# Inverse square roots by powers on GpSimd, the second FFN product in three f32r parts, and a new order of steps in a graph attention kernel

## The chip, the core and the metric

The kernel runs on one core of one Trainium2 chip, in one launch. The metric is the device time in microseconds, median of the runs. A core has TensorE (PE; its weight loads are PEld), VectorE (DVE), ScalarE (ACT), GpSimd (POOL), and SyncE (SP), which here only issues DMAs. Each engine takes its instructions in the order written and waits on semaphores for the others.

## The reference

There are N = 10000 nodes with 512 features and E = 5000 edges, sorted by `dst`. Only the first block is run (one layer), and its result is normalized once more:

```python
q = (h @ Wq).reshape(n, 8, 64); k = (h @ Wk).reshape(n, 8, 64); v = (h @ Wv).reshape(n, 8, 64)
e = einsum('ehd,ehd->eh', k[src], q[dst]) / sqrt(64)
ex = exp(e - segment_max(e, dst)[dst]);  attn = ex / segment_sum(ex, dst)[dst]
a = segment_sum(attn[:, :, None] * v[src], dst).reshape(n, 512)
x1 = layernorm(h + a @ Wo, ln1_g, ln1_b)
f = relu(x1 @ W1 + b1) @ W2 + b2            # 512 -> 64 -> 512
y = layernorm(x1 + f, ln2_g, ln2_b)
out = layernorm(h + y)                      # no gain or bias; eps 1e-5 everywhere
```

A layer norm needs 1/sqrt(var + eps) of each row, three times for each node.

## The kernel before

**Rounds.** The edges are taken in ten rounds of 500 (four tiles of 125 rows). In a round the rows x[dst] and x[src] are gathered by indirect DMAs (`GXD`, `GXS`, four each), turned on TensorE (`TXD0` to `TXD3`, `TXS0` to `TXS3`, line 1023), and split into a rounded part and a rest in the f32r type (ScalarE line 519, VectorE line 759). The products with Wq, Wk, Wv and Wo (`Q0`..`Q3`, `K`, `V`, `O`; line 963) are each 4 chunks x 3 f32r matmuls (hi x hi, lo x hi, hi x lo). Softmax over a segment is done by scans along the edges (lines 784, 802, 838). `H0`..`H3` (line 821) add x[dst] to the O product.

**Jobs.** All that follows attention is done in four slots a round: N0 and N1 take nodes that no edge reaches (250 rows each), E0 and E1 take the rows of the edges. A slot's pass is called a job, so there are 40. Its steps are: `sum`/`mv` or `m1` (mean), `sd` (deviation), `r1` (reciprocal), `norm`, `T` (turning on TensorE, line 1059), `F1` (first FFN product, plain f32, line 1095), `F2` (second, plain f32: two matmuls with 64 rows of contraction, one on partitions 0 to 63 and one on 64 to 127, each into its own bank, line 1103), `xr`, `x2` (line 898, adds the FFN's result), `sq` (squares, line 558), `t`, `r2`, `y` (line 917), `sq3`, `r3`, `z` (the last norm) and `out` (two scatters). GpSimd issues all gathers and scatters, and `be`, a DMA that adds ln2's bias.

**The deviations.** ScalarE computes Sqrt(var + eps) of a 125x2 tile (line 550) and VectorE its reciprocal (line 856). Exp and Ln are in another table set than Sqrt, so that each round loads a set before its softmax (line 521) and the other one after it (line 533).

**The FFN's banks.** For a job ScalarE seeds one bank with zeros (line 609) and one with the bias (line 610); after `F1` it takes Relu with bias b1 into `hT` (line 600) and then seeds the first bank with the bias (line 602). The last three jobs have steps of their own (`B9`, `F19`, `F29`, lines 1072 to 1088).

**The start.** The indices are cast, turned by three small transposes (`TURN`, lines 972 and 975), and written to tables (`TABS`, line 675 and on). `TABS` stands behind all casts and behind `FLAG` on VectorE. GpSimd's constants (lines 398 to 409) stand ahead of `GXD`. SyncE issues the loads of Wq and Wk before those of b1 and W1, and that of Wv when the x[dst] rows are there. `COUNT0`..`COUNT4` (line 999), `ROFF` and `LIST` make the list of the nodes without an edge.

**The order.** `PLAN` gives each step of each engine a due time; `sequence(engine)` sorts by them, and the engine's block issues the steps in that order. Rounds 2 to 7 of the ten share one set of times, shifted by a period. `FILLERS` names steps behind which TensorE does idle matmuls on `below` (line 1116): 27 are in the start and in the closing jobs, 31 behind steps of round 8.

Of the kernel before, what the change touches and what calls it, by code (L numbers as in the profile page):

```python
# [21 lines left out]
PERIOD = 7684  # L22
SLOT_PERIOD = {"N0": 7687, "N1": 7689}
PLAN = {
    "pe": """
!TURN -276034; !FOLD -51782; !OFFS -237181; !TURNF -205187; !COUNT0 -202748; !COUNT1 -198663; !COUNT2 -146723;
!COUNT3 -94502; !COUNT4 -90190; !ROFF -71911; !BITS -8816; TXD0 -189819 -22912 125030 125323 125345;
TXS0 -102406 26305 131951 131437 131817; Q0 -138628 34546 131782 132194 129672; K0 -59911 65956 133983 133320 137209;
V0 27356 105501 136738 136738 170605; O0 89451 141151 143013 157654 247834; TXD1 -186065 -14365 126120 126712 125690;
TXS1 -100425 38188 132022 131705 131969; Q1 -106115 57936 132236 132221 132162; K1 -40813 69908 134313 133555 140512;  # L30
V1 33080 113889 136894 136880 181017; O1 106767 141614 143149 165755 248144; TXD2 -166405 -7868 129028 130799 126518;
TXS2 -88980 41299 132413 132381 134849; Q2 -86792 64359 132527 132551 134538; K2 -30166 75112 134486 134513 140777;
V2 33666 129876 137553 138275 190162; O2 109181 144067 143559 170305 254002; TXD3 -155949 21677 129100 130978 126648;
TXS3 -83495 62551 132620 132450 134986; Q3 -70414 73944 132661 132967 137118; K3 -18228 75867 134696 134659 145042;
V3 35699 134599 138141 140689 197551; O3 120150 144307 144103 175555 259059; S -2195 93578 135748 135731 159438;
<N0.T 145667 146316 145309 195433 299769; >N0.T9 136827 117852 145308 201617 306764;
>N0.B9 134375 173381 147765 210695 422904; >N0.F19 113824 134962 147690 188156 364727;
>N0.F29 123023 126945 148591 190152 461807; <N0.F1 147630 147818 147691 210881 382824;
<N0.F2 148607 149380 148592 224978 338963; N1.T 102574 142344 143517 152979 224183;
N1.F1 111204 143358 143969 159019 234579; N1.F2 115493 144385 144312 165751 254378;  # L40
<E0.T 122067 143089 144266 177444 355474; >E0.T9 160739 161239 144265 204642 261163;
>E0.B9 93219 141972 144577 202312 260912; >E0.F19 251340 193305 144554 229074 272138;
>E0.F29 116239 128247 144888 201657 275488; <E0.F1 141560 144900 144555 177658 271119;
<E0.F2 142460 145428 144889 179837 216780; <E1.T 143829 145481 144995 216690 280606;
>E1.T9 156254 161915 144994 210970 295480; >E1.B9 154640 155450 145824 230013 303813;
>E1.F19 150032 151466 145585 214520 312915; >E1.F29 121122 181510 146664 236757 339253;
<E1.F1 145525 146724 145586 230812 332624; <E1.F2 146622 147196 146665 235181 341159
""",
    "act": """
!HQ -295440; !HK -89319; !HV -61854; !HO -45097; TXD0 -171196 -18312 125712 127231 125178;  # L50
TXS0 -68603 20337 131158 130993 132478; Q0 -111138 42579 131621 131004 131070; V0 27197 127292 136963 137699 161962;
TXD1 -146012 -9176 126544 127368 125657; TXS1 -67208 29303 131398 131008 132770; Q1 -73839 60821 132277 131401 133090;
V1 37750 130738 138269 138390 173142; TXD2 -137214 -5075 128839 130614 126389; TXS2 -65419 35207 132157 131352 133268;
Q2 -17185 62273 132574 132889 134345; V2 62190 138918 139637 142583 207890; TXD3 -118766 8616 128915 130664 126472;
TXS3 -48877 52021 132497 132466 133316; Q3 -10791 71890 132992 133126 134392; V3 74728 140001 140381 145994 218182;
S 3247 92165 136014 135911 153062; LN 5242 95004 136180 136183 156284; XP 19875 106412 136396 136399 158334;
N0.sd 123676 144544 144342 152828 256165; N0.norm 139316 145803 144558 162385 274768;
<N0.T 145914 146124 145919 169837 375832; >N0.T9 183982 167878 145918 179401 296352;
>N0.F19 139706 158972 147088 149539 310138; <N0.seed 146645 147058 146583 176207 232821;
<N0.F1 147225 148612 147089 177596 315363; N0.sq 148176 149711 149081 215130 338403;  # L60
N0.sq3 150792 150053 150194 238119 450805; <N0.z 151547 150704 150711 263169 440476;
N1.sd 79021 140055 141467 142403 189027; N1.norm 95949 140381 142614 146272 196458;
N1.T 102191 142631 143102 147994 208475; N1.seed 77479 140669 142165 147282 218765;
N1.F1 109626 143603 143753 154439 220364; N1.sq 125334 145685 145585 156964 246118;
N1.sq3 143159 146401 146231 166158 297324; N1.z 146052 147623 148527 175369 319246;
E0.sd 116445 141882 143068 154716 239656; <E0.norm 130307 141972 143719 160108 226853;
<E0.T 133834 143647 144061 161814 186592; >E0.T9 200185 167176 144060 163787 257027;
>E0.F19 127976 159096 144422 167136 271087; <E0.seed 124355 144129 144234 162277 258999;
<E0.F1 140883 144817 144423 165883 237520; E0.sq 146290 146220 146119 168507 281215;
E0.sq3 147174 148677 147797 184383 337581; E0.z 147692 149932 149758 196327 349547;  # L70
E1.sd 132863 144633 144278 166339 260324; <E1.norm 136923 145071 144498 176344 204613;
<E1.T 143222 145930 144586 186840 203336; >E1.T9 157259 128692 144585 225796 279483;
>E1.F19 150692 123805 145647 214704 292567; <E1.seed 143985 146062 145367 199873 298615;
<E1.F1 144354 146133 145648 207445 312511; E1.sq 147924 147214 146670 227666 327598;
E1.sq3 148558 148885 149937 229129 359991; <E1.z 149166 150501 150260 232611 340778
""",
    "dve": """
!CAST -263381; !FLAG -243336; !TABS -242836; !FILLI -241863; !FW -55094; !B1 -55229; !LQ -172721; !LK -85485;
!LV -54432; !LO 76605; !CNT0 -198287; !CNT1 -179760; !CNT2 -159099; !CNT3 -97504; !CNT4 -91086; !RANK -79616;
!DIG -211902; !LIST -79575; TXD0 -162172 -29587 125840 127315 124482; TXS0 -89151 40059 130890 130776 132032;  # L80
K0 -51732 66249 133633 132533 134452; W0 18249 122663 136307 136222 169476; N0 35421 125323 136834 136488 170118;
G0 49521 129368 137409 137177 185919; L0 44048 128784 137153 137940 187035; H0 89910 140875 142983 151481 211814;
TXD1 -161904 -24476 126177 127482 124895; TXS1 -88968 56437 131385 130810 132286;
# [77 lines left out]
def graph_attention(nc, x, src, dst, Wq, Wk, Wv, Wo, g1, be1, g2, be2, W1, b1, W2, b2, out):  # L161
# [15 lines left out]
    with ctx:  # L177
# [125 lines left out]
        def hidden(i, slot):  # L303
            n = closing.index((i, slot))
            return pS[:, R * n:R * n + R]
# [4 lines left out]
        def pT_of(i, step, half=0):  # L310
            return pT[turn[i, step, half] % 2]
# [829 lines left out]
```

## Time and profile before

| | |
|---|---|
| three runs | 683.09, 683.85, 684.23 us; median 683.85 |
| profiled execution | span 682.0 us from first to last instruction; the page gives no separate device time for it, so that the median lies 1.85 us above this span |
| PE | 641.5 us busy, 94% |
| DVE | 578.0 us, 85% |
| ACT | 528.3 us, 77% |
| POOL | 401.7 us, 59% |
| DMA | 91.44 MB, mean 134 GB/s |
| granted TensorE clock | 0.986 on average |

Busy times are unions, so two instructions that run side by side count once. A group's mean is that of one instruction. A plain f32 matmul leaves two records in this profile and an f32r matmul one: the 80 F2 matmuls are 160 records, 12 of them in lines of the closing jobs.

### The profile page before, as it was taken

To read this page: it belongs to the slowest core of one execution; us is meant where nothing else is said; L and a number is where in the kernel's file an instruction comes from. 1 tells how busy PE (TensorE), PEld (TensorE's weight loads), DVE (VectorE), ACT (ScalarE), POOL (GpSimd) and SP (SyncE) were. 2 spreads that over 40 slices of the span, in tenths; PEclk is the share of its full clock that TensorE was granted. 3 is DMA by queue.
4 is the path that set the end of the run, shared out by engine and by line. 5 is a ranking of instruction groups with operands and counts; after the bars stand their busy time and mean duration, and the time that the engine had idled before them with its cause. 6 is when DMAs were issued, how large, how long until landed. Compare 5 with 4: busy or idle time off the path is not lost. (4 is left out here: it accounts for less than half of the span.)

```text
span 682.0 us, 10864 instructions
## 1 busy us (share of the span) xinstructions
PE 641.5 (94%) x3520; PEld 483.8 (71%) x3520; DVE 578.0 (85%) x1391; ACT 528.3 (77%) x1140; POOL 401.7 (59%) x363
## 2 busy tenths in 40 slices
PE   5999999999999999999999999999999999999950
PEld 2778877777777777777777777777778778675520
DVE  7668769879898898898889889988989898899792
ACT  2525269877888987988798889878878999698881
POOL 7267244867675865756776574864547726735423
PEclk9999999999999999999999999999999999999995
DMA  7844154644643745674474456455554824536452
GB/s 227 220 101 133 44 123 106 173 122 142 148 121 131 159 121 148 167 157 92 146 177 117 113 161 137 105 168 123 127 128 155 184 62 135 139 77 138 131 113 91
DMA packets 37747, 91.44 MB, mean 134 GB/s; under 512 B 8346, under 2 KB 9642, under 8 KB 37690
## 3 DMA queue, kind: packets, MB, share of 16 engines
q0 software_dynamic: 31536, 82.74, 47.6%
q1 hardware_dynamic: 6154, 8.01, 4.3%
q8 instruction: 28, 0.46, 0.3%
q14 instruction: 29, 0.24, 0.1%
HBM read 71.20 MB, written 20.99 MB: 135 GB/s over the span
## 5 line engine op out<-in xcount | busy, mean ns | idle before, releaser
L558 ACT ACTIVATE squares<-rows,nmean 125x512 bf16<-125x512 f32 x200 | 142.3, 713 | 41.5 <-DVE nmean L902 19.8
L412 POOL DMA_INDIRECT x_rows<-in_x_dram,node_idx x40 | 48.2, 1205 | 56.8 <-DVE rows L917 47.3
L416 POOL DMA_INDIRECT out_dram<-rows,node_idx x40 | 46.4, 1160 | 56.4 <-ACT rows L618 47.0
L473 POOL DMA_DIRECT2D x_rows<-in_L_gnn_ln_b_dram x40 | 52.9, 1372 | 31.1 <-DVE rows L821 21.7
L898 DVE SCALAR_TENSOR_TENSOR rows<-pF,rows 125x512 f32<-125x512 f32 x78 | 50.6, 686 | 23.2 <-PE pF L1103 22.5
L963 PE MATMUL pP<-wo_hi,aT_hi 128*125 128x512 f32 x160 | 65.9, 412 | 0.3 <-DVE aT_lo L848 0.3
L963 PE MATMUL pP<-xTs_hi,wv_hi 128*128 128x500 f32 x160 | 65.8, 411 | 0.0
L963 PE MATMUL pP<-xTd_hi,wq_hi 128*128 128x500 f32 x160 | 65.4, 409 | 0.1
L963 PE MATMUL pP<-xTs_hi,wk_hi 128*128 128x500 f32 x160 | 63.5, 397 | 0.6 <-ACT q L539 0.6
L963 PE MATMUL pP<-wo_lo,aT_hi 128*125 128x512 f32 x160 | 63.1, 394 | 0.0
L963 PE MATMUL pP<-wo_hi,aT_lo 128*125 128x512 f32 x160 | 63.0, 394 | 0.0
L416 POOL DMA_INDIRECT out_dram<-rows,edge_idx x40 | 43.5, 1086 | 33.1 <-ACT rows L618 23.8
L963 PE MATMUL pP<-xTs_hi,wk_lo 128*128 128x500 f32 x160 | 62.4, 390 | 0.0
L963 PE MATMUL pP<-xTs_hi,wv_lo 128*128 128x500 f32 x160 | 62.3, 390 | 0.0
L963 PE MATMUL pP<-xTd_lo,wq_hi 128*128 128x500 f32 x160 | 62.3, 390 | 0.0
L963 PE MATMUL pP<-xTd_hi,wq_lo 128*128 128x500 f32 x160 | 62.2, 389 | 0.0
L963 PE MATMUL pP<-xTs_lo,wv_hi 128*128 128x500 f32 x160 | 62.2, 388 | 0.0
L963 PE MATMUL pP<-xTs_lo,wk_hi 128*128 128x500 f32 x160 | 62.1, 388 | 0.0
L412 POOL DMA_INDIRECT x_rows<-in_x_dram,edge_idx x40 | 44.5, 1113 | 28.1 <-issue 11.3
L618 ACT ACTIVATE rows<-rows,shift,rs 125x512 f32<-125x512 f32 x76 | 57.4, 805 | 1.4 <-DVE shift L933 1.4
L917 DVE SCALAR_TENSOR_TENSOR rows<-rows,rs,x_rows 125x512 f32<-125x512 f32 x80 | 57.1, 750 | 0.9 <-DMA x_rows<-in_L_gnn_ln_b_dram 0.7
L907 DVE SCALAR_TENSOR_TENSOR rows<-rows,nmean,g_all 125x512 f32<-125x512 f32 x80 | 57.6, 761 | 0.1
(197 smaller groups left out, 1760.6 us busy)
## 6 DMA issues: line engine op xcount, KB each, us to landing
x_rows<-in_L_gnn_ln_b_dram POOLq DMA_DIRECT2D x40, 512.0 KB, 6.7
dst_row<-in_dst_dram SPq DMA_DIRECT2D x9, 250.5 KB
q<-in_L_gnn_Wq_dram SPq DMA_DIRECT2D x1, 1024.0 KB, 5.6
rows<-in_L_gnn_Wk_dram SPq DMA_DIRECT2D x1, 1024.0 KB, 7.8
rows<-in_L_gnn_Wv_dram SPq DMA_DIRECT2D x1, 1024.0 KB, 6.8
x_rows<-in_L_gnn_Wo_dram SPq DMA_DIRECT2D x8, 128.0 KB, 6.0
xd<-in_x_dram,dst_idx POOLq DMA_INDIRECT x40, 4.6
xs<-in_x_dram,src_idx POOLq DMA_INDIRECT x40, 3.8
```

The lines of the kernel that those rows point to most:

```text
L412: pool.indirect_dma_start(rows, None, x, bass.IndirectOffsetOnAxis(ap=table[:, column:column + 1].bitcast(U32), axis=0), bounds_check=N - ...
L416: pool.indirect_dma_start(out, bass.IndirectOffsetOnAxis(ap=table[:, column:column + 1].bitcast(U32), axis=0), rows, None, bounds_check=N ...
L473: pool.dma_start(xr_wide[n], bass.AP(tensor=be2.tensor, offset=be2.offset, ap=[[0, P], [0, 2], [1, D]]), accum_op=ALU.add).then_inc(s[f"be ...
L558: ins = act.activation(squares[:, t, :], w[n][:, t, :], ACT.Square, bias=nmean[c][n][:, t:t + 1], accum_out=sq[c][n][:, t:t + 1])
L618: ins = act.activation(w[n][:, t, :], w[n][:, t, :], ACT.Identity, scale=rs[3][n][:, t:t + 1], bias=shift[n][:, t:t + 1])
L898: dve.scalar_tensor_tensor(w[n][:, t, :], f_banks(i, slot)[t][0:R, :], 1.0, w[n][:, t, :], ALU.mult, ALU.add, accum_out=sums[2][n][:, t:t ...
L907: ins = dve.scalar_tensor_tensor(w[n][:, t, :], w[n][:, t, :], nmean[2][n][:, t:t + 1], g2_all[0:R, :], ALU.add, ALU.mult)
L917: ins = dve.scalar_tensor_tensor(w[n][:, t, :], w[n][:, t, :], rs[2][n][:, t:t + 1], xr[n][:, t, :], ALU.mult, ALU.add, accum_out=sums[3][ ...
L963: ins = pe.matmul(acc, left(a, k), right(b, k), start=(k == 0 and a == b), stop=(k == KC - 1 and a == 1))
```

## The change

**Powers on GpSimd.** `sd`, `r2` and the reciprocals of `r1` and `r3` go, and both table loads of each round. New POOL steps `p1`, `p2`, `p3` do two small instructions each: var = scale * x + eps, then var to the power -0.5. One table set is loaded at the start. The bias b1 is put into the seeded bank, so that Relu has none.

```diff
-    act.activation(sd[c][n][:, :], var, ACT.Sqrt, bias=eps_col[0:R, :], scale=scale).then_inc(s[f"sd{c}"], 1)
-    dve.reciprocal(rs[c][n][:, :], sd[c][n][:, :]).then_inc(s[f"rs{c}"], 1)
+    if what in ("p1", "p2", "p3"):                                    # GpSimd
+        if what == "p1" and slot[0] == "N":
+            on.wait_ge("mv_done", 2 * nth("dve.mv", slot, i))
+            pool.tensor_scalar(var[c][n][:, :], mv[n][:, :, 1], 1.0, EPS, ALU.mult, ALU.add).then_inc(s[f"var{c}"], 1)
+        else:
+            on.wait_ge(f"sq{c}", nth(f"act.sq{c}", slot, i))
+            pool.tensor_scalar(var[c][n][:, :], sq[c][n][:, :], 1.0 / D, EPS, ALU.mult, ALU.add).then_inc(s[f"var{c}"], 1)
+        on.wait_ge(f"var{c}", nth(f"pool.p{c}", slot, i))
+        pool.tensor_tensor(rs[c][n][:, :], var[c][n][:, :], minus_half[0:R, :], ALU.pow).then_inc(s[f"rs{c}"], 1)
-                act.preload_act_table_set(tables)
-                act.preload_act_table(ACT.Sqrt)
```

**F2 as three f32r products.** W2 is split into hi and lo at the start (`FHI` on ScalarE, `FLO` on VectorE), `hT` in each job (Relu writes hi, the new VectorE step `lo` the rest). The bank that `F1` used is seeded in a step of its own (`seed1`) behind `lo`.

```diff
-    for t in range(2):
-        pe.matmul(pF[1 - t][0:R, :], hT[DFF * t:DFF * t + DFF, :], w2[DFF * t:DFF * t + DFF, :], ...)
+    on.wait_ge("h_lo", nth("dve.lo", slot, i))
+    for a, b in ((0, 0), (1, 0), (0, 1)):
+        for t in range(2):
+            half = slice(DFF * t, DFF * t + DFF)
+            ins = pe.matmul(f_banks(i, slot)[t][0:R, :], hT[a][half, :], w2[b][half, :], start=False, stop=(b == 1), ...)
+    dve.scalar_tensor_tensor(hT[1][:, :], hidden(i, slot), 0.0, hT[0][:, :].bitcast(F32), ALU.max, ALU.subtract)
```

**Gathers first.** `TURN`, `CAST` and `TABS` are cut in two, so that the dst table is written right behind its own cast and transpose. `GXD` stands ahead of GpSimd's later constants (now step `INIT`), `GXS` behind them. SyncE issues Wk (and W2 ahead of it) when x[dst] is there, and Wv when x[src] is there.

**Tile-wise turning.** `TXDt` and `TXSt` now turn tile t (125 rows, all four chunks) and not chunk k of all tiles, and wait for that tile's gather alone; each gather of the next round waits for its own tile's turning.

```diff
-    on.wait_ge(f"{which}_loaded", 64 * (i + 1))
-    for t in range(4):
-        ins = pe.transpose(pT_of(i, step)[:, R * t:R * t + R], rows[0:R, t, P * k:P * k + P], ident[0:R, 0:R])
+    on.wait_ge(f"{which}_loaded_{t}", 16 * (i + 1))
+    for k in range(KC):
+        ins = pe.transpose(pT_of(i, step)[:, R * k:R * k + R], rows[0:R, t, P * k:P * k + P], ident[0:R, 0:R])
```

**The order.** `PLAN` has a time for each step of each of the ten rounds; the sum of the steps is the same but for those named. The due times are in another unit than before. The first PE steps are now TURN1, TURN2, OFFS, TURNF, TXD0, TXD1, TXD2, FOLD, TXD3, Q0, TXS0, COUNT0, COUNT1 (before: TURN, OFFS, TURNF, COUNT0, COUNT1, TXD0 to TXD3, COUNT2, Q0). Three closing jobs (E0, N0, E1 of round 9) still follow the last product O3. `FILLERS` now has 24 idle matmuls, all in the start.

**Smaller.** The row of dst values shares its memory with `weight`, and its load for the next round waits for `log_taken` instead of `mask_eq`. Of the three closing jobs E0 and E1 of round 9 keep `B9`; N0 goes the ordinary way. The index fill has one semaphore a round.

## Rows read from the trace of the kernel before

**Rows 1.** The page's first part: busy us, share of the span, instructions

```profile
PE 641.5 (94%) x3520; PEld 483.8 (71%) x3520; DVE 578.0 (85%) x1391; ACT 528.3 (77%) x1140; POOL 401.7 (59%) x363
```

**Rows 2.** Stretches of the span; columns as named in its first line

```profile
core 0: us, PE busy (x) PEld busy (x) DVE busy (x) ACT busy (x) POOL busy (x), PEclk, DMA share, GB/s
0.00:21.00 21.00, 12.31 (x68) 6.72 (x68) 16.09 (x47) 5.71 (x9) 13.95 (x29) 1.00 0.79 245
268.00:329.00 61.00, 61.00 (x338) 46.63 (x337) 54.13 (x131) 52.15 (x115) 40.51 (x34) 1.00 0.56 139
594.00:640.00 46.00, 43.07 (x243) 28.91 (x242) 40.78 (x105) 41.89 (x97) 21.71 (x18) 1.00 0.47 113
640.00:682.00 42.00, 15.27 (x101) 7.94 (x99) 26.86 (x79) 23.77 (x59) 14.13 (x13) 0.78 0.37 99
```

**Rows 3.** The chain that ended last, from 630 us on, by line

```profile
by line: ACT squares L558 22.2%; issue 11.2%; ACT rows L618 8.6%; POOL out_dram L416 5.4%; DVE rows L917 5.2%; DVE rows L898 4.9%; ACT sd L550 4.6%; DVE rows L886 3.2%; DVE rows L892 3.0%; DVE st L865 2.3%; DVE rows L926 2.2%; ACT nT L586 2
```

**Rows 4.** Timeline of TensorE in a middle round: start us, length us, instruction

```profile
305.45 0.39 PE L963 MATMUL pP<-xTs_hi,wv_lo 128*128 128x500 f32 x1
305.77 1.13 PE L1103 MATMUL pF<-w,hT 64*125 64x512 f32 x4
306.83 0.49 PE L963 MATMUL pP<-xTd_hi,wq_hi 128*128 128x500 f32 x1
307.16 0.38 PE L963 MATMUL pP<-xTd_lo,wq_hi 128*128 128x500 f32 x1
```

**Rows 5.** Groups by line: busy us, mean ns of one | idle us before

```profile
L1103 PE MATMUL pF<-w,hT 64*125 64x512 f32 x148 | 41.7, 640 | 0.0
L1030 PE MATMUL pS<-q,same_head 128*128 128x500 f32 x20 | 10.3, 596 | 0.3 <-DVE q L771 0.3
L1116 PE MATMUL pS<-below 128*128 128x512 bf16 x31 | 7.2, 380 | 0.0
```

**Rows 6.** Timeline of TensorE at the start

```profile
2.80 0.40 PE L972 MATMUL pF<-ident,ex 40*125 40x40 f32 x1 [2.80 <-DVE ex L655]
15.81 1.07 PE L1023 MATMUL pT<-ident,xd 125*128 125x125 f32 x8 [1.22 <-DMA xd<-in_x_dram,dst_idx]
19.77 0.69 PE L999 MATMUL pS<-x_rows 125*128 125x80 bf16 x8
20.98 0.47 PE L963 MATMUL pP<-xTd_hi,wq_hi 128*128 128x500 f32 x1
...
38.41 0.89 PE L982 MATMUL pF<-be_col,nsame 128*64 128x1 f32 x16
```

**Rows 7.** Timelines at the start, of VectorE and of GpSimd

```profile
2.35 0.31 DVE L655 CAST ex<-ex 40x125 f32<-40x125 int32 x1 [1.17 <-DMA ex<-in_dst_dram]
...
6.54 0.18 DVE L675 CAST dst_idx<-pF 125x40 int32<-125x40 f32 x1
...
7.68 1.21 POOL L412 DMA_INDIRECT xd<-in_x_dram,dst_idx  x1 [1.80 <-DVE is_last L680]
...
11.82 1.12 POOL L412 DMA_INDIRECT xd<-in_x_dram,dst_idx  x1 [0.31 <-issue]
```

**Rows 8.** Groups by line of ScalarE and VectorE

```profile
L550 ACT ACTIVATE sd<-sq,eps_col 125x2 f32<-125x2 f32 x100 | 29.6, 296 | 3.2
...
L521 ACT ACT_TABLE_LOAD x10 | 12.8, 1283 | 0.2
...
L856 DVE RECIPROCAL rs<-sd 125x2 f32<-125x2 f32 x120 | 18.9, 158 | 13.8 <-ACT sd L550 13.4
```

**Rows 9.** Two lines alone: duration in ns, min/median/max

```profile
L892 DVE TENSOR_TENSOR rows<-rows,g_all x40: 1198/1217/1558, 96.8 to 652.0; 125x1024 f32<-125x1024 f32 x40
...
L459 POOL TENSOR_SCALAR far<-nsame x10: 598/992/1481, 48.4 to 586.5; 128x500 f32<-128x500 f32 x10
```

**Rows 10.** Timelines in a middle round, VectorE and GpSimd

```profile
239.75 1.55 DVE L892 TENSOR_TENSOR rows<-rows,g_all 125x1024 f32<-125x1024 f32 x1
...
238.75 1.48 POOL L459 TENSOR_SCALAR far<-nsame 128x500 f32<-128x500 f32 x1 [0.36 <-DVE nsame L766]
```

More of the change, by code:

```diff
@@ L290, in graph_attention @@
         pe_steps = sequence("pe")
-        turns = [(i, step, half) for i, step in pe_steps if step[:2] == "TX" or step.endswith((".T", ".T9"))
+        turns = [(i, step, half) for i, step in pe_steps if step[:2] == "TX" or step.endswith(".T")
                  for half in range(1 if step[:2] == "TX" else 2)]
@@ L318, in job_before, with banks_before @@
             return jobs[n - 1] if n else None
+        def banks_before(i, slot):
+            earlier = [one for one in jobs[:job[i, slot]] if one != closing[1]]
+            return earlier[-1] if earlier else None
         steps_done = {}
-        for engine in ("pe", "act", "dve"):
+        for engine in ("pe", "act", "dve", "pool"):
             done = {}
@@ L588, in _ @@
                                 .then_inc(s["nT_done"], 1)
-                    elif what == "F19":
-                        before = job_before(i, slot)
-                        on.wait_ge("f_filled", 2 * nth("pe.F2", before[1], before[0]))
-                        on.wait_ge("h_filled", nth("pe.F1", slot, i))
-                        act.activation(hT[:, :], hidden(i, slot), ACT.Relu, bias=b1_col[:, :]).then_inc(s["h_done"], 1)
                     elif what == "F1":
@@ L888, in _ @@
                         ins.then_inc(s["last_n1_done"], 1)
+                    elif what == "lo":
+                        on.wait_ge("h_done", nth("act.F1", slot, i))
+                        dve.scalar_tensor_tensor(hT[1][:, :], hidden(i, slot), 0.0, hT[0][:, :].bitcast(F32), ALU.max, ALU.subtract)\
+                            .then_inc(s["h_lo"], 1)
                     elif what == "xr":
@@ L1098, in _ @@
                     elif what == "F2":
[L1099 to L1104 removed]
+                        on.wait_ge("w2_lo", 1)
+                        on.wait_ge("h_lo", nth("dve.lo", slot, i))
+                        if (i, slot) not in closing:
+                            on.wait_ge("seeded_0", nth("act.seed", slot, i))
+                            on.wait_ge("seeded_1", nth("act.seed", slot, i))
+                        for a, b in ((0, 0), (1, 0), (0, 1)):
+                            for t in range(2):
+                                half = slice(DFF * t, DFF * t + DFF)
+                                ins = pe.matmul(f_banks(i, slot)[t][0:R, :], hT[a][half, :], w2[b][half, :],
+                                                start=False, stop=(b == 1), skip_group_check=True)
+                                if b == 1:
+                                    ins.then_inc(s["f_filled"], 1)
                 if idle:
```

463 lines of the change are left out of this document (238 added, 225 removed).

## The prediction

> **What bounds the kernel now.** I read the page's busy times first: TensorE is busy in 94% of the span [rows 1]. A union over ten rounds hides differing stages, so I then cut the span. Four stages show [rows 2]. In the first 21 us TensorE is busy for only 12.3, part of that idle matmuls. In a middle round it is busy for 61.0 of 61 us: TensorE alone sets the pace, while VectorE has 6.9 us left and ScalarE 8.9. From 594 to 640 us TensorE is busy 43.1 of 46, but 7.2 of these are the idle matmuls behind round 8's steps [rows 5], so it really waits for 2.9 + 7.2 = 10.1 us; VectorE and ScalarE are busy 40.8 and 41.9. From 640 us on the closing jobs run, and TensorE has little to do. The chain there [rows 3] is ScalarE's squares (22%) and last norm (9%), VectorE's row steps, and scatters. So a gain has to come from the start, from TensorE's work in the rounds, or from the ScalarE and VectorE chain after 594. What only relieves ScalarE in a middle round is worth nothing.
>
> **Start.** The dst table's cast ends at 2.66 us and its transpose at 3.20 [rows 6, 7], but the table is written at 6.54 to 6.72, and the first gather starts at 7.68, 0.96 behind it [rows 7]. With the table written right behind its transpose (0.18 more, 3.4 us) and the same 0.96, the first gather starts at 4.4, 3.3 earlier; the fourth would start at 11.82 - 3.3 = 8.5. TensorE could turn the first rows at 15.81, when all four tiles were there: 4.0 after the last gather's start. The last tile is then there at 12.5, and less if the Wk load that no longer runs beside it had slowed it; bounds 11.5 and 14. Before, all turning, splitting and counting between 15.81 and the first product took 5.2 us [rows 6]. Tile-wise, only the last tile's turning is behind the last landing: four transposes (half of the 1.07 for eight), then one ScalarE and one VectorE pass. The transposes are 0.54; a pass over 500 columns is about half of the 1.22 us for 1024 [rows 9], so two are 1.3 with a little of hand-off: 2.0 in all. FOLD (0.89) stands ahead of the last turning and waits for W1; for it I add 0.3. The first product starts at 14.8 (13.5 to 17.5) instead of 20.98, 6.2 earlier. But three counting steps like that at 19.77 [rows 6], about 0.6 each where they overlap, now come after it, +1.9, and FOLD before it, -0.9. Net -5.2 (bounds -7 and -1).
> GpSimd's queue: `INIT` moved behind GXD keeps the x[src] gathers at about 13 us, as before. Cover for them is Q0 to Q3 (12 matmuls of 0.23 each, 11 us) and the counts. Wk is issued some 10 us later than before and has those same 11 us and the turning; if this cover failed, each late us would cost one.
>
> **F2.** In the middle round F2 starts at 305.77 and the next product at 306.83: 1.06 us for two plain f32 matmuls of 512 columns [rows 4]. The two run side by side: 148 records of 640 ns make 94.7 us but a union of 41.7, whereas the score's f32 matmuls (20 of 596 ns, 11.9 us) have a union of 10.3 [rows 5]. The new F2 has six f32r matmuls in three pairs. An f32r matmul takes 0.23 us from start to start (307.16 less 306.83 is 0.33, the first after a change of shape, and 305.45 is followed after 0.32, so a change costs about 0.1 on either side). Side by side: 0.33 + 0.23 + 0.33 = 0.89, a gain of 0.17. In turn: 0.33 + 4 x 0.23 + 0.33 = 1.58, a loss of 0.52. No row shows two f32r matmuls of 64 rows; the nearest is the same pair of 64-row tiles in f32, so I take 0.89. The 148 records are 37 jobs, all before the closing three: 37 x 0.17 = -6.3 (bounds -6.3 and +19).
> The step between Relu and F2, VectorE's `lo` (a 125-column pass; nearest rows 0.16 for 2 columns [rows 8] and 1.22 for 1024 [rows 9], I take 0.3), is hidden by products that stand between in a round. Uncovered it adds 0.35 with its hand-off.
>
> **Sqrt and reciprocal.** Gone from ScalarE: 100 x 0.296 and 20 of about the same length, 35 us, and twenty table loads of 1.28, 25.7 us; from VectorE 18.9 us busy and 13.8 of waiting [rows 8]. In rounds 1 to 8 this is off the path: nothing. GpSimd gets 24 small instructions a round. Their time is not in the trace. It lies above nothing and, for 2 elements, should be below the 0.60 that 500 elements take at best [rows 9], unless a power costs much more for each element than a multiply. The pair takes the place of 0.30 + 0.16 us; I take 0.5 for it, with both hand-offs, so that a single chain is as long as before (bounds 0.2 and 1.5).
> GpSimd has room: busy 40.5 of 61 us [rows 2], and 28 indirect DMAs a round with 0.3 of issue ahead of each [rows 7] make 8.4 more, so 12.1 are free for 12 pairs: 1.0 us each. A pair stands in order with the gathers, though, and a `p` step that waits for ScalarE's squares holds back the gathers and scatters written behind it. These have a round of slack in the middle.
> GpSimd's passes also slow VectorE's: the 1024-element product takes 1.56 us while GpSimd's 500-element pass runs, against a median of 1.22 [rows 9, 10]. The new instructions are far smaller; 24 of 0.25 us, hitting VectorE's two-input passes a third of the time, cost it 2 us a round, within its 6.9 us of slack. The Trainium skill, "SBUF — State Buffer", section "SBUF: two separate sides", says that the loser of the port shared by GpSimd and VectorE blocks for the whole instruction, only where VectorE has two SBUF inputs and GpSimd reads SBUF. By that rule the saving of the reciprocals could be eaten up; the trace shows a delay of 0.34, not the whole 1.48 us, and even the whole rule leaves the middle rounds bound by TensorE.
>
> **594 to 640 us.** TensorE's 10.1 us of waiting are given by the chain of the other two. VectorE's 40.8 of 46 us allow 5.2 less at most if its work stays; ScalarE loses in this stretch, with about four jobs' worth of three Sqrt each, 3.6 us and a table load (1.3) and the waits of reciprocals on them. The new order spreads the jobs of round 8 otherwise, which no row prices. I take -5.2 (bounds 0 and -12).
>
> **Closing jobs and the last scatters.** On the chain, Sqrt is 4.6% of 52 us, 2.4 us [rows 3], and the reciprocal's part goes with it; the power pairs take that place. ScalarE's own queue is relieved by 0.3 a step where squares follow squares (-1.5), three F2 save 0.5, and two or three `lo` add 0.35 each (+0.8). Net -1.2, bounds -5 and +4.
>
> **Sum.** 682.0 - 5.2 - 6.3 - 5.2 - 1.2 = 664.1 us of span. The median of the runs is 1.85 above the profiled span; the same distance gives 665.9. I predict 665.5.
>
> **Rivals.**
> (A) The f32r pairs run in turn. The 37 F2 then cost +19 in place of -6.3: 665.5 + 25.5 = 691, slower. It decides from the point where F2's slot is over 1.06 + 11.6/37 = 1.37 us. For it: f32r is another mode, and no row has it in 64 rows. Against: the f32 pair already overlaps. Chance 0.07.
> (B) GpSimd becomes the bound: a pair costs over 1.0 us, gathers and scatters come late, and TensorE idles. At 1.3 us a pair a round is 12 x 0.3 = 3.6 longer, over eight rounds +29: 694. It is slower than before from a pair of 1.2 us on. For it: a power by software can be costly, and the queue is in order. Against: two elements only. Chance 0.10.
> (C) The idle matmuls of round 8 are gone and TensorE pauses there still. The granted clock is 1.00 from 594 to 640 and 0.78 in the stretch after [rows 2]. If it falls to 1.2 GHz before the last four O products (48 x 0.23 = 11 us), these take twice as long, but three of these products can lie in time that others need: +6, 672. Chance 0.10.
> (D) The new order does all that it can: TensorE's 10.1 us go wholly, the start gives 7, the closing 4: 682.0 - 7 - 6.3 - 10.1 - 4 + 1.85 = 656. Chance 0.23.
>
> **Chances.** The forecast has 0.50, its own range 659 to 673. With C and D and the small part of the forecast's tail, faster by over 0.2% (about what a measurement of this kernel tells from no change) has 0.82, within 0.2% 0.04, slower 0.14. The range from 650 to 682 takes in D with margin, and C, and leaves out A and the worse part of B.
>
> **What would show it.** Start: the first of the Q products at about 14.8 us, first gather at 4.4. F2: a union of its records of about 0.9 to 1.0 us and 0.89 from its start to the next product's; 1.58 would be A. GpSimd: the pair's two durations, and its busy time in a middle round under 52 us a round; TensorE idle in the middle behind gathers would be B. The period of a round, from one mask step on GpSimd to the next, gets 0.7 us shorter. TensorE's granted clock under 1 before the last O product would be C. I am wrong if the period doesn't fall, or if the stretch from the last V product to the end is no shorter than before.

## The result, and the profile after

The changed kernel takes 757.58 us (median of 4 runs, 754.92 to 759.89) against 684.04 us beside it on the same chip: 1.107 times as long, 95% interval 1.1041 to 1.1099. The forecast was 665.5, its range ended at 682. The profiled span is 753.0 us.

The page after has these rows: busy times, the shares of the chain that ended last, and the two instructions of a power step (the second is the power). The columns are those of [rows 1, 5].

```profile
PE 648.0 (86%) x3562; PEld 496.6 (66%) x3562; DVE 570.0 (76%) x1310; ACT 477.9 (63%) x1008; POOL 535.0 (71%) x603
...
POOL 47%; issue 25%; DVE 11%; PE 7%; ACT 6%; DMA 3%; POOLq 1%; DVEq 0%; ACTq 0%
...
L509 POOL TENSOR_TENSOR rs<-var,minus_half 125x2 f32<-125x2 f32 x120 | 98.9, 824 | 10.2 <-issue 0.2
L506 POOL TENSOR_SCALAR var<-sq 125x2 f32<-125x2 f32 x100 | 28.7, 287 | 34.1 <-ACT squares L600 28.1
```

TensorE does as much as before (648 us against 641.5 [rows 1]) in 71 us more of span: nothing got more work for it, it waits. The chain that ended last now goes back through the whole span: GpSimd holds 47% of it, and most of "issue" stands ahead of GpSimd's instructions. For the kernel before, the profile follows this chain only through the last part [rows 3], where it was ScalarE's and VectorE's, so the two are not compared further. Stretches of the span after, with the columns of [rows 2]; the last one, from 85 to 590 us, takes all middle rounds together, and the row under it is the same stretch of the kernel before:

```profile
0.00:21.00 21.00, 12.59 (x65) 6.74 (x66) 11.99 (x47) 5.83 (x9) 15.66 (x32) 1.00 0.68 225
268.00:329.00 61.00, 55.04 (x317) 41.66 (x316) 46.28 (x109) 40.99 (x89) 44.09 (x51) 1.00 0.47 126
660.00:700.00 40.00, 31.40 (x172) 23.29 (x168) 32.47 (x82) 29.94 (x67) 26.42 (x30) 0.87 0.38 97
700.00:753.00 53.00, 17.05 (x98) 9.99 (x98) 25.52 (x68) 25.75 (x58) 28.57 (x39) 0.66 0.33 92
...
85.00:590.00 505.00, 461.94 (x2534) 357.39 (x2533) 391.60 (x885) 336.60 (x710) 373.66 (x414) 0.98 0.49 125
```

```profile
85.00:590.00 505.00, 503.82 (x2771) 384.89 (x2770) 444.36 (x1070) 427.61 (x925) 315.94 (x271) 1.00 0.54 137
```

From 85 to 590 us TensorE was busy for 503.8 of 505 us before and for 461.9 now. The round, taken from the first Q product of round 1 to that of round 9 and divided by eight, was 60.1 us (63.0 to 543.6) and is 67.7 (51.1 to 592.7). The last O product ends at 699.9 instead of 639.2, and what follows takes 53.2 us instead of 42.8. So 61 us of the 71 are lost before the last O product and 10 behind it.

Who waits for the powers is seen in the waits of the changed kernel (us in total, times, longest):

```profile
DVE shift L971 <- POOL rs L509: 49.6, 30, 3.2
POOL x_rows L430 <- DVE rows L956: 34.5, 15, 3.7
POOL var L506 <- ACT squares L600: 28.1, 22, 3.2
DVE nb L914 <- POOL rs L509: 19.9, 15, 3.3
```

I read this as a ring: VectorE waits for a power, the power's queue waits for ScalarE's squares, and the gather behind it waits for VectorE's rows. In a middle round GpSimd's timeline has both kinds in one queue:

```profile
289.54 1.00 POOL L434 DMA_INDIRECT out_dram<-rows,edge_idx  x1 [0.30 <-issue]
290.61 0.19 POOL L506 TENSOR_SCALAR var<-sq 125x2 f32<-125x2 f32 x1
290.88 0.72 POOL L509 TENSOR_TENSOR rs<-var,minus_half 125x2 f32<-125x2 f32 x1
291.69 0.19 POOL L503 TENSOR_SCALAR var<-mv 125x2 f32<-125x2 f32 x1
291.97 1.03 POOL L509 TENSOR_TENSOR rs<-var,minus_half 125x2 f32<-125x2 f32 x1
293.98 1.13 POOL L430 DMA_INDIRECT x_rows<-in_x_dram,edge_idx  x1 [0.98 <-DVE rows L956]
```

At best a step takes 1.0 us from 290.61 to 291.60; over all of them it is 0.29 + 0.08 between the two + 0.82 = 1.19 us.

### The profile page after: what moved, and what is told of

Same layout as the page of the kernel before. It is cut to its first block, busy times and chain, and to the rows that moved or that the text cites. A ratio compares the mean times of both kernels' runs of the same rounds, so it can differ in the third digit from the quotient of the medians.

```text
span 753.0 us, 11117 instructions
## 1 busy us (share of the span) xinstructions
PE 648.0 (86%) x3562; PEld 496.6 (66%) x3562; DVE 570.0 (76%) x1310; ACT 477.9 (63%) x1008; POOL 535.0 (71%) x603
## 4 chain that ended last, share of the span: by engine, by line
POOL 47%; issue 25%; DVE 11%; PE 7%; ACT 6%; DMA 3%; POOLq 1%; DVEq 0%; ACTq 0%
POOL x_rows L430 10%; POOL rs L509 8%; POOL out_dram L434 8%; POOL x_rows L518 5%; POOL edge_idx L486 4%; POOL xs L430 4%; PE pP L1001 4%; POOL xd L430 4%; POOL var L506 3%; DVE rows L956 3%; ACT squares L600 3%; DVE rows L939 2%; DVE att L880 1%; DVE rows L948 1%; PE pT L1062 1%
## 5 line engine op out<-in xcount | busy, mean ns | idle before, releaser
L509 POOL TENSOR_TENSOR rs<-var,minus_half 125x2 f32<-125x2 f32 x120 | 98.9, 824 | 10.2 <-issue 0.2
L653 ACT ACTIVATE rows<-rows,shift,rs 125x512 f32<-125x512 f32 x78 | 59.2, 807 | 31.4 <-DVE shift L971 31.4
L430 POOL DMA_INDIRECT x_rows<-in_x_dram,node_idx x40 | 50.4, 1259 | 31.2 <-DVE rows L956 20.8
L1001 PE MATMUL pP<-wo_hi,aT_hi 128*125 128x512 f32 x160 | 68.5, 428 | 0.0
L1098 PE MATMUL pT<-ident,rows 125*128 125x125 f32 x320 | 45.1, 285 | 26.7 <-ACT rows L612 14.1
L434 POOL DMA_INDIRECT out_dram<-rows,edge_idx x40 | 48.6, 1214 | 26.6 <-ACT rows L653 16.1
L1001 PE MATMUL pP<-xTs_hi,wk_hi 128*128 128x500 f32 x160 | 65.3, 408 | 1.0 <-issue 0.7
L430 POOL DMA_INDIRECT x_rows<-in_x_dram,edge_idx x40 | 45.7, 1144 | 23.3 <-DVE rows L956 13.7
```

The costliest lines, as they stand in the source:

```text
L430: pool.indirect_dma_start(rows, None, x, bass.IndirectOffsetOnAxis(ap=table[:, column:column + 1].bitcast(U32), axis=0), bounds_check=N - ...
L434: pool.indirect_dma_start(out, bass.IndirectOffsetOnAxis(ap=table[:, column:column + 1].bitcast(U32), axis=0), rows, None, bounds_check=N ...
L509: pool.tensor_tensor(rs[c][n][:, :], var[c][n][:, :], minus_half[0:R, :], ALU.pow).then_inc(s[f"rs{c}"], 1)
L653: ins = act.activation(w[n][:, t, :], w[n][:, t, :], ACT.Identity, scale=rs[3][n][:, t:t + 1], bias=shift[n][:, t:t + 1])
L1001: ins = pe.matmul(acc, left(a, k), right(b, k), start=(k == 0 and a == b), stop=(k == KC - 1 and a == 1))
L1098: ins = pe.transpose(pT_of(i, step, half)[:, 2 * R * c + R * t:2 * R * c + R * t + R], w[n][:, t, P * (2 * half + c):P * (2 * half + c) + ...
```

## The experiments

Each ratio is to the kernel before, beside it on the same chip. "Points" are hundredths of the time before (6.84 us). Kernels that were measured at different times are compared by their ratios.

**e1_mult.** The changed kernel without the power: a multiply of the same tiles stands in its place, and all waits stay.

```
-pool.tensor_tensor(rs[c][n][:, :], var[c][n][:, :], minus_half[0:R, :], ALU.pow)
+pool.tensor_tensor(rs[c][n][:, :], var[c][n][:, :], minus_half[0:R, :], ALU.mult)
```

> The changed kernel with the power on GpSimd replaced by a multiply of the same 125x2 tiles; its place in the queue and all waits stay (the norms are then wrong by this factor). Theory D (the power's own duration, 0.82 us against about 0.27 for a small multiply, fills GpSimd's in-order queue): 120 x 0.55 = 66 us of GpSimd work go, and the time falls by most of the loss, to 680 to 700 us. Rival W (not the duration, but that steps that wait for ScalarE now stand in the gathers' queue): hardly faster, 735 to 757. Rival O (order and start of the changed kernel are what is slow): 745 to 757.

726.25 us, ratio 1.054 (1.0499 to 1.0581). The same row as above now reads

```profile
L509 POOL TENSOR_TENSOR rs<-var,minus_half 125x2 f32<-125x2 f32 x120 | 35.8, 299 | 10.2 <-issue 0.2
```

so a step costs 0.29 + 0.08 + 0.30 = 0.67 us. Taking 0.52 us out of each of 120 steps gives back 5.3 points, 36 us. The other half of the loss stays although a step, at 0.67 us, is now near the 0.5 that the forecast took.

**e2_sqrt.** The new order with ScalarE's Sqrt and VectorE's reciprocal back, where the powers' inputs end.

```
+act.activation(var[c][n][:, :], var_in, ACT.Sqrt, bias=eps_col[0:R, :], scale=scale)   # ScalarE, behind the squares
+dve.reciprocal(rs[c][n][:, :], var[c][n][:, :])                                       # VectorE, where it waited for GpSimd
-pool: N0.p1 ... E1.p3
```

> The changed kernel with Sqrt on ScalarE and reciprocals on VectorE again, all else kept; because the new order puts 14 of the Sqrt inside the softmax, there are up to 14 more pairs of table loads than before (about 36 us of ScalarE). Theory D or W: 660 to 690 us, faster than or equal to before. Rival O: 735 to 757.

760.26 us, ratio 1.1047 (1.1001 to 1.1094). Neither theory expected this. The new order lays norms between a softmax's Exp and Ln, so the trace has 44 table loads of 1.283 us against 21 before (ten of them in [rows 8]). This is no clean undoing; e3 is. The Trainium skill, "ScalarE: Activation LUTs", section "What ACT_TABLE_LOAD costs", gives a switch 1283 ns and some 1380 more for draining. The trace agrees on the 1283; no row shows the rest. Against e3, which has a single table set and no reciprocals, e2 loses 5.2 points or 35 us for 43 more loads and the reciprocals. That is 0.8 us a load net; e3 has 120 short activations more (24.5 us busy), and with all of those on the path it would be 1.4. Part of the 35 us is the clock (below).

**e3_lnexp.** The new order, with nothing of the norms on GpSimd: exp(-0.5 ln v), both in the softmax's table set.

```
+act.activation(var[c][n][:, :], var_in, ACT.Ln, bias=eps_col[0:R, :], scale=scale)
+act.activation(rs[c][n][:, :], var[c][n][:, :], ACT.Exp, scale=-0.5)
-pool: N0.p1 ... E1.p3
```

> The changed kernel with each inverse root as exp(-0.5 ln(x)) on ScalarE, two small activations in the one table set that the softmax uses, nothing on GpSimd or VectorE. Theory D or W: 655 to 675 us, the forecast's sum without its power term, faster than before. Rival O: 735 to 757.

726.28 us, ratio 1.0529 (1.0479 to 1.0579), the same as e1 within its interval. Steps of 0.67 us on GpSimd cost the same as none there with 120 more short activations on ScalarE; powers of 1.19 cost 5.4 points more (4.8 to 6.0). But the expectation of 655 to 675 was off by 50 us: without any power on GpSimd the kernel is still 5.3 points slower.

**e4_before_pow.** The order of before on TensorE, ScalarE and VectorE, with the powers on GpSimd put where the Sqrt ran in the trace of before.

```
+pool.tensor_scalar(sd[c][n][:, :], sq[c][n][:, :], 1.0 / D, EPS, ALU.mult, ALU.add)
+pool.tensor_tensor(rs[c][n][:, :], sd[c][n][:, :], minus_half[0:R, :], ALU.pow)
-act Sqrt, dve.reciprocal, table loads
```

> The kernel before, in its own order, with only the powers moved to GpSimd (no Sqrt, no table loads, no reciprocals); each pair stands in GpSimd's queue where the Sqrt ran in the trace of before. Theory D or W: the loss comes with this part alone, 725 to 770 us. Rival O: 670 to 690.

788.39 us, ratio 1.1462 (1.1416 to 1.1508). This one edit alone, in the old order, costs 14.6 points: more than the whole change. With powers on GpSimd, the new order and the other parts together (10.7) do better than the old order alone (14.6); whether the old order would do as well with the powers at other places of GpSimd's queue was not run.

**e5 to e8.** The other parts in the order of before, one by one and together.

```
e5  -ACT.Sqrt, dve.reciprocal, preload_act_table       +ACT.Ln, ACT.Exp (scale=-0.5)
e6  -pe.matmul(pF[1 - t], hT, w2)                      +for a, b in ((0, 0), (1, 0), (0, 1)): pe.matmul(pF[1 - t], hT[a], w2[b])
    +dve: hT[1] = max(pF, 0) - hT[0]                   +b1 in the seeded bank; the other bank's seed waits for h_lo
    +the closing three jobs leave out hT[1]            +dst_row shares weight's memory; +wait_ge("log_taken", i) ahead of its load
e7  -pe.transpose(rows[:, t, chunk k]) for t           +for k; gathers with a semaphore for each tile
e8  e5 + e6 + e7
```

> The kernel before with its own order on every engine; only the inverse deviation is computed otherwise: exp(-0.5 ln(v + eps)) as two small ScalarE activations in the place of each Sqrt, no reciprocal on VectorE, and none of the twenty table loads. Theory O (the new order of steps is what costs the changed kernel the some 40 us that stay without powers): this one stays near before, 678 to 686, since its middle rounds stay full on TensorE. Theory C (a chain of a norm became longer wherever the Sqrt is replaced, and the rounds hang on it): 700 or more, and TensorE waits behind ScalarE's norm in the rounds.

700.12 us, ratio 1.0197 (1.0172 to 1.0222). Between the two theories. From round 4 on the rounds are as before (61.7 us against 61.5); 13.0 of the 15.1 us at the last O product are lost by then. The timelines show the largest piece, and TensorE's stretch the granted clock (the mean is 0.97) under 1:

```profile
124.80 1.22 PE L1058 MATMUL pT<-ident,rows 125*128 125x125 f32 x8 [0.34 <-issue]
129.20 0.37 ACT L602 ACTIVATE hT<-pF,b_col 128x125 f32<-128x125 f32 x1 [4.59 <-remote]
130.34 2.07 PE L1102 MATMUL pF<-w,hT 64*125 64x512 f32 x4 [4.33 <-issue]
...
85.00:150.00 65.00, 59.87 (x326) 44.78 (x325) 48.07 (x106) 46.22 (x107) 30.57 (x27) 0.97 0.54 132
```

The matmuls of the second product, side by side 1.1 us before [rows 4], take 2.07 behind that pause. The pause isn't ScalarE's: Relu waits for the semaphore that F1's last matmul raises, and the trace has that event at 129.11, 4.7 us behind the matmul's recorded end (124.45; such ends are modelled in the profile); in the kernel before the same two are 0.03 us apart in that round. Why TensorE reports so late isn't known, so these 4 us are not shown to come from a chain that got longer.

> The kernel before with only the second FFN product changed: three f32r products of split h and W2 (VectorE's lo pass put where the trace of before has the Relu's end, b1 seeded in the bank, dst_row sharing weight's memory as in the changed kernel, so a round's row load waits for the logarithm of the round before). The closing three jobs leave out the product with h's low part. Theory O: TensorE gains 0.17 us in each of 37 jobs, so 677 to 683. Theory F (the edit costs elsewhere: the lo pass stands in VectorE's queue, the seed waits for it, the row load comes late): 690 or more.

696.67 us, ratio 1.0164 (1.0134 to 1.0194): the edit that was to give 6.3 us costs 11. The rounds are 62.1 us long. The stretch from 268 to 329, and ScalarE's longest wait from 300 to 600 us:

```profile
268.00:329.00 61.00, 59.94 (x344) 46.90 (x343) 54.15 (x133) 51.66 (x114) 39.44 (x34) 1.00 0.56 138
...
ACT pF L611 <- DVE hT_lo L873: 18.5, 17, 2.3
```

In the middle rounds of before, F2 starts 1.3 to 2.4 us behind the Relu's end for three jobs of four. A low part that queues behind a VectorE step, and the bank's seed behind it, may not fit into that; e10 tests it.

> The kernel before with only the turning made tile-wise: each transposing step turns one tile's four chunks and waits for that tile's gather alone, each gather waits for its own tile. Order and start otherwise as before. Theory O: no measurable change in the rounds, at most 1 to 2 us off the start: 681 to 687. Theory T (tile-wise turning delays the gathers or the product): 692 or more.

689.03 us, ratio 1.0031 (1.0008 to 1.0053): a small loss. The first product comes 1.6 us earlier (19.40) and the K product waits 4.1 us for ScalarE's copy of Q.

> The three parts of the three kernels beside it together in before's order: exp and ln for Sqrt and reciprocal, three f32r products, tile-wise turning (the closing three jobs leave out the product with h's low part). It differs from e3_lnexp in the order of the steps, the start and the fillers alone. Theory O: 670 to 682, some 45 us under e3_lnexp's 726. Theory C, F or T: near e3_lnexp, over 710.

711.2 us, ratio 1.0339 (1.0299 to 1.0379). The three parts add up within their intervals: 1.97 + 1.64 + 0.31 = 3.9 points, 3.4 measured (3.0 to 3.8). They don't lose where e6 lost, though: the middle rounds are 61.3 us, as before, and 22 of the 29 us that the profiled run is late at the last O product are lost by the start of round 4. Theory O expected no loss here, and is wrong for the greater part: e3's 5.3 points are 3.4 for the parts and only 1.9 (1.3 to 2.5) for what e3 has besides, the new order with its start, the other idle matmuls, and the low part in the closing jobs.

**e10_before_no_lo.** e6 without the low part of h.

```
-for a, b in ((0, 0), (1, 0), (0, 1)):      -dve "lo" steps; the seed waits for the Relu alone
+for a, b in ((0, 0), (0, 1)):
```

> e6_before_f2 without VectorE's lo pass and without the product that uses it (two f32r products a job in the place of three; h's low part is left out of the result). Theory L (the lo pass between Relu and second product is what lengthened e6's rounds, as ScalarE's seed and TensorE's product wait for VectorE's queue): the round gets shorter than before's 61.4 us, by up to 0.17 + 0.23 = 0.4 us a job, so 672 to 680. Rival R (the shared memory of dst_row and weight, or the seeding, costs it): it stays at 690 or more, with rounds of 62 us.

680.39 us, ratio 0.9921 (0.9889 to 0.9953). The rounds are 60.6 us (305.8 to 366.4 to 426.9) with the shared row memory and the new seeding still there. A third f32r pair is 0.23 us, 37 of them 8.5; the other 8 of the 16 us between e6 and e10 (by the two intervals 3 us either way) go with the low pass and the waits for it. That isn't all of the miss. With two pairs in place of the f32 product, F2 should give 1.6 us a round (4 x 0.40), and its time from start to start does fall from 4.23 to 2.65; but the round gives 0.9. TensorE never stood in such a round of before. Here it stands for 0.63 us ahead of a turning (second line), and in e6 for 0.38 (first line):

```profile
318.18 0.65 PE L1040 MATMUL pT<-ident,xs 125*128 125x125 f32 x4 [0.38 <-DVE xTs_lo L772]
...
313.99 0.65 PE L1040 MATMUL pT<-ident,xs 125*128 125x125 f32 x4 [0.63 <-issue]
```

So of the 17 us between the forecast for F2 (-6.3) and e6 (+11), some 8 are the low pass with its waits, and some 9 stay with what e10 keeps: the seeding, the row memory, or an order that was laid out for the old lengths. No run tells these apart. The expected 672 to 680 was just missed.

**e11_before_first.** Only the gathers first, weights loaded as before.

```
 dve.tensor_copy(idx_f[0:CT, 1, :], idx_raw[0:CT, 1, :])
+on.wait_ge("idx_turned", 1)
+dve.tensor_copy(dst_idx[0:R, :], pF[0][0:R, 0:CT])
-pool.iota(...), memset(...)   # ahead of the loop; now behind the first GXD
```

> The kernel before with only the gathers put first: the dst table is written right behind its transpose, and GpSimd's later setting up moves behind the first four gathers; weights are loaded where they were. The first gather should start at 4.4 us instead of 7.7, and the first Q product some 2 to 3 us earlier. Theory S (an earlier start is worth its time, since TensorE is full from then on): 681 to 684. Rival (what follows is held by weights, counts and the first softmax, or a pause there lowers the clock, as in e7): 687 or more.

684.78 us, ratio 0.9991 (0.9973 to 1.0009): nothing. GpSimd's first and fourth gather; then VectorE, TensorE, and TensorE's clock:

```profile
4.47 1.26 POOL L399 DMA_INDIRECT xd<-in_x_dram,dst_idx  x1 [1.49 <-DVE dst_idx L658]
...
8.69 1.00 POOL L399 DMA_INDIRECT xd<-in_x_dram,dst_idx  x1 [0.30 <-issue]
...
12.52 0.69 DVE L646 TENSOR_TENSOR x_rows<-nT,att 125x1024 bf16<-125x1024 bf16 x1 [3.78 <-POOL att L421]
...
14.00 0.75 PE L999 MATMUL pS<-x_rows 125*128 125x80 bf16 x8 [3.78 <-DVE x_rows L646]
...
16.79 1.87 PE L1023 MATMUL pT<-ident,xd 125*128 125x125 f32 x8
...
16.70:18.70 2.00, 2.00 (x10) 1.75 (x9) 1.21 (x3) 0.59 (x2) 1.55 (x2) 0.50 0.91 307
...
22.74 0.47 PE L963 MATMUL pP<-xTd_hi,wq_hi 128*128 128x500 f32 x1
```

The gathers start 3.2 us earlier [rows 7], and the last landing that the trace has is at 14.60 (57 of 64 events are there; before, the last is at 15.77). Yet the rows are turned 1.0 us later than before [rows 6]. TensorE isn't waiting for rows, it is busy without a break from 14.00 on. What is late is the work ahead of the turning: GpSimd's constants now stand behind the gathers, VectorE waits 3.78 us for them, and TensorE's counting step, which stands ahead of the turning, starts at 14.00 instead of 12.13. Behind that pause the granted clock is 0.50, the lower level, so that eight transposes take 1.87 us against 1.07.

**e12_after_hold.** Idle matmuls in TensorE's pauses of the changed kernel.

```
+HOLD = {(0, 'Q0'): 22, (0, 'E1.T'): 8, ..., (8, 'S'): 8}
+if (i, step) in HOLD: bank_free(*next turn); for _ in range(HOLD[i, step]): pe.matmul(pT, below, below)
```

> The changed kernel with 123 idle matmuls (0.23 us each, into a transpose bank that is free then) ahead of 14 steps at which TensorE waited 1.2 to 5.3 us: ahead of Q0 of round 0 and of 13 steps of the rounds. Nothing else is changed, and each filling is no longer than the wait that it stands in. Theory H (the waits cost twice: once as idle time and again as a lower granted clock behind them, 10.2 us of full-speed work lost between 21 and 641 us): the clock stays at 1.00 in most of the places and the time falls by 6 to 10 us, 747 to 752. Rival: the clock's loss is hidden by other waits, or the idle matmuls delay the work: 756 or more.

771.16 us, ratio 1.1242 (1.1194 to 1.129): 1.7 points slower than the changed kernel. The clock is 1.00 from 21 to 85 us instead of 0.97, but summed up to 641 us (as below) 13.7 us of it are lost against 10.2: it falls behind other steps. Theory H isn't borne out as a way to win the time back; what the clock costs by itself stays an account from the trace.

**e13_after_pow_one.** The power of one column, a multiply for the other.

```
-pool.tensor_tensor(rs[:, :], var[:, :], minus_half, ALU.pow)
+pool.tensor_tensor(rs[:, 0:1], ..., ALU.pow);  pool.tensor_tensor(rs[:, 1:2], ..., ALU.mult)
```

> The changed kernel with the power of 125 x 2 cut in two instructions: a power of one column, and a multiply of the other (so the second tile of each pair gets a wrong deviation). It is run for the durations alone. If a power costs mostly by the element, the one-column power takes about half of the 0.72 us median above the 0.29 us of a plain pass, 0.45 to 0.55; if it costs a fixed amount, 0.65 or more. The time as a whole: near the changed kernel's, 750 to 765, as 0.3 us of a multiply is added and as much taken away.

758.96 us in one run. The two groups:

```profile
L509 POOL TENSOR_TENSOR rs<-var,minus_half 125x1 f32<-125x1 f32 x120 | 80.8, 674 | 10.2 <-issue 0.2
L510 POOL TENSOR_TENSOR rs<-var,minus_half 125x1 f32<-125x1 f32 x120 | 28.6, 239 | 0.0
```

The means hold some instructions that took over 1 us. The medians (middle figure) of the power with one column, of the multiply with one, and of the power with two in the changed kernel are cleaner:

```profile
L509 POOL TENSOR_TENSOR rs<-var,minus_half x120: 548/571/1442, 65.4 to 743.2; 125x1 f32<-125x1 f32 x120
L510 POOL TENSOR_TENSOR rs<-var,minus_half x120: 179/181/1094, 65.9 to 743.8; 125x1 f32<-125x1 f32 x120
...
L509 POOL TENSOR_TENSOR rs<-var,minus_half x120: 689/723/1658, 64.1 to 739.2; 125x2 f32<-125x2 f32 x120
```

So a second column costs a power 152 ns, and 419 stand before any column. A multiply has 181 and, in e1, 197: 16 and 165. The greater part of the power's price is fixed. That is why "two elements only" was no argument.

**The account, in points of 684 us.** Inverse roots on ScalarE without Sqrt, f32r and tiles in the old order 3.4 (e8); the new order and start 1.9 (e3 less e8); powers at their real price on GpSimd 5.4 (the change less e3): 10.7. The last two terms are differences of two kernels, each known to some 0.6 points. What the new order alone does isn't shown by a run of its own.

## Why the prediction was wrong

**The step that failed first: "I take 0.5 for it"**, for a power pair on GpSimd. It is 1.19 us, within the bounds of 0.2 and 1.5 but beyond the 1.0 for which I had found room. Rival (B), given 0.10, is the nearest to what happened, and it named 1.2 us as the point of "slower than before". I came to 0.5 from "should be below the 0.60 that 500 elements take at best", the argument by size that e13 takes away. At 0.67 us (e1) GpSimd costs nothing against e3, at 1.19 it costs 37 us; where between them the loss begins no run shows. The size of the rival was short: by its arithmetic 12 x 0.19 us over eight rounds make 18 us. And its mechanism, a GpSimd without room, isn't what the trace has: from 268 to 329 us GpSimd is busy for 44.1 of 61. That is 49 for a round of 67.7 us, under the 52 that I had named as the sign against (B), and with 8.4 of issue it leaves 10 us free. Still GpSimd stands and waits for VectorE's rows and ScalarE's squares. What fits is an order that passes each delay on to the gathers behind it; the waits above show both kinds, but no run takes the ring apart.

In all, 92 us lie between the forecast and the measurement: 37 are the powers' price, and the other 55 are a kernel that without it (e3) came 36 us slower than before, where the sum had it 18 faster. With a step of 0.67 us (e1) the kernel is still 5.4 points slower, so the power's price alone doesn't explain the miss.

The page on GpSimd in the Trainium skill, "GPSIMD Engine Reference", section "3.1 Elementwise — side-by-side cycle accounting", says that each instruction there pays two software hops of dispatch and about 2.6 cycles an element. The trace agrees that there is a fixed part: 165 ns for a multiply by the medians of e13 and e1. For a power it is 419. The figure for an element can't be seen in one or two columns.

**"In rounds 1 to 8 this is off the path: nothing"** failed even for a cheap replacement. In the old order, ln and exp cost 13 us (e5), nearly all of it before round 4, while the rounds from 4 on are as long as before. So the middle rounds did have the room, and the first ones hadn't: round 0 is 3.1 us longer and round 1 6.7. Of these, 4.3 are the stop at 130 us, whose cause is open, and 3.4 over the whole are clock (below). Which chain lost the rest wasn't found.

**F2.** The slot is right: 397.48 to 398.37 is 0.89 us, and the pairs run side by side.

```profile
397.48 0.49 PE L1132 MATMUL pF<-w_hi,hT_hi 64*125 64x512 f32 x2
397.81 0.40 PE L1132 MATMUL pF<-w_hi,hT_lo 64*125 64x512 f32 x2
398.04 0.40 PE L1132 MATMUL pF<-w_lo,hT_hi 64*125 64x512 f32 x2
398.37 0.49 PE L1001 MATMUL pP<-xTd_hi,wq_hi 128*128 128x500 f32 x1
```

Rival (A) is out. `lo` is 281 ns in the median, as taken (0.3). What failed is "is hidden by products that stand between in a round": by e6 and e10 it isn't, and costs some 8 us. The forecast's -6.3 was +11 in the old order; the other 9 of these 17 us belong to no term of the sum, since seeding and row memory stood in it at nothing.

**The start.** The first gather is at 4.56 (4.4 forecast), the last tile has landed at 12.97 (12.5 forecast), the last turning starts at 14.35, but Q0 at 20.30 and not at 14.8. The timeline of TensorE, and below it ScalarE's pass over the last tile:

```profile
14.35 0.62 PE L1062 MATMUL pT<-ident,xd 125*128 125x125 f32 x4
14.80 1.24 PE L1147 MATMUL pP<-below 128*128 128x512 bf16 x5
20.30 0.47 PE L1001 MATMUL pP<-xTd_hi,wq_hi 128*128 128x500 f32 x1 [4.25 <-issue]
...
18.89 0.59 ACT L566 ACTIVATE xTd_hi<-pT 128x500 fp32r<-128x500 f32 x1 [4.82 <-remote]
```

ScalarE starts 3.9 us behind the recorded end of the turning (14.96). It waits for the semaphore that the turning raises, and the trace has this event at 18.87; for the three tiles before, it comes 0.01 us behind the turning's end. So it is TensorE that reports late, as in e5. In e3, the same code up to there, the event is at 15.99 and Q0 at 17.41. What holds TensorE's report is open. Further on the late Wk shows: the first K product is at 38.06 against 35.60, the first score at 53.91 against 49.89. I had counted the start from its first product alone; by the score, which the first softmax needs, it is 4 us later than before.

**594 to 640, and closing.** These -5.2 and -1.2 had no row. From the last V product to the end it is 82.9 us instead of 71.2, and 10.3 of the 11.7 us stand behind the last O product. That part is 42.8 us before, 44.7 in e8, 49.6 in e3 and 53.2 in the changed kernel: some 2 for the parts, 5 for the new order with the low part in the closing jobs, 4 for the powers. The powers themselves are 11.5% of the chain from 700 us on, 6 us, where the kernel before had Sqrt and reciprocals.

**The clock, rival (C),** came in its place, with little effect, and in others. From 676 to 687 us the granted clock is 0.53, behind pauses of 3.2 and 3.8 us; only the first two of the last four O products' 48 matmuls fall into it, some 0.4 us. In the middle rounds, where it was 1.00 before, it fell too. Around a pause at 147 us the timeline reads

```profile
146.70 0.40 PE L1001 MATMUL pP<-wo_hi,aT_lo 128*125 128x512 f32 x1
149.10 1.08 PE L1120 MATMUL pF<-nT,w 128*64 128x125 f32 x16 [2.01 <-ACT pF L644]
150.85 0.78 PE L1001 MATMUL pP<-xTs_hi,wk_hi 128*128 128x500 f32 x1 [0.67 <-issue]
151.43 0.62 PE L1001 MATMUL pP<-xTs_lo,wk_hi 128*128 128x500 f32 x1
151.84 0.62 PE L1001 MATMUL pP<-xTs_hi,wk_lo 128*128 128x500 f32 x1
```

The last two are 0.41 us apart instead of 0.23: the lower level, 1.2 GHz. From 21 to 641 us, one less the clock summed over 62 stretches of 10 us makes 10.2 us in the changed kernel, 9.9 in e1, 13.6 in e3, 10.2 in e8, 28.9 in e2, 23.8 in e4, 3.4 in e5 and e7, 0.0 in before and e6. This is the most of full-speed work that it can have cost, as TensorE also idles in such stretches. So a pause can be paid twice. These are single traces: over the four runs of the changed kernel the mean clock goes from 0.944 to 0.956, and the profiled run has the highest. e12 shows that filling the known pauses doesn't get it back.

**VectorE's delay.** I took the 0.34 us of [rows 9, 10] as speaking against a block for the whole instruction. It doesn't: VectorE's pass started at 239.75, 1.00 us into GpSimd's 1.48, and only 0.48 were left to wait for. Where I quoted the Trainium skill ("SBUF — State Buffer", section "SBUF: two separate sides"), I wrote "only" and left out its other case, a VectorE instruction in a two-port mode. Neither changes the sum.

**The signs I named.** The period was to get 0.7 us shorter and got 7.6 longer. The last V product to the end was to get shorter and got 11.7 longer. Both said that I was wrong.

What this came to: the forecast treated the order as free ("The new order spreads the jobs of round 8 otherwise, which no row prices") and priced each part against the sums of a round. All three parts, priced at a gain or nothing, lose in the order of before.

## What to carry to other kernels

- Where an engine is busy for 61.0 of 61 us, its in-order queue is fitted to when each input comes. A rewrite on another engine is then better priced by the latency from its input to its user, step by step, against the slack before that user, than by busy time. Here a product that is 0.17 us shorter in each of 37 jobs came with a new pass of 0.28 us, another seeding and another memory for a row, and the kernel lost 11 us instead of gaining 6.3.
- Don't price an operation that no row shows by the number of its elements. Here one run with one power in it would have told 0.7 to 0.8 us.
- A queue with both gathers and small arithmetic that others wait for can become a ring. Its free time in a round isn't enough to ask for (here 44.1 of 61 us were busy): ask what each late arithmetic step does to the gathers behind it.
- Moving a step forward moves others back. In e11 the gathers came earlier and the counting steps later, and TensorE's queue had the counting steps first.

## What the runs showed of the hardware

- A GpSimd power of 125 x 2 takes 824 ns in the mean (689 to 1658, median 723), a multiply 299 (median 197, e1), a power of 125 x 1 674 (median 571, e13).
- Three pairs of f32r matmuls of 64 rows and 512 columns run side by side: 0.89 us from the first start to the next product.
- Pauses of TensorE of about 2 us were followed by the lower clock at some times and not at others. Of the twelve of 1.9 to 3.0 us between 63 and 593 us in the changed kernel, it fell after five (they end at 149, 174, 334, 468 and 572 us) and not after seven (66, 135, 203, 252 with 3.0 us, 418, 537, 592).
- Four gathers that start 3.2 us earlier beside two weight loads have their last recorded landing 1.2 us earlier (e11, 14.60 against 15.77).
- TensorE's semaphore events mostly come 0.01 to 0.03 us behind the recorded end of the matmul, but some come late: 4.7 us in e5 (F1, at 129.11), 3.9 in the start of the changed kernel (the last turning, at 18.87), 1.3 at the same place of e3. The engine that waits shows "remote" or "issue". The cause wasn't found.
